# The fp4 network of a two-layer program: VectorE does the whole rounding of the wide row, and the turn is reordered

## The reference, cut to what matters

```python
def fp4_quant_dequant(x):               # blocks of 16 along the last dimension
    xb = x.reshape(shape[:-1] + (shape[-1] // BLOCK, BLOCK))
    scale = jnp.max(jnp.abs(xb), axis=-1, keepdims=True) / 6.0
    scale = jnp.maximum(scale, jnp.float32(1e-12))
    xn = xb / scale
    idx = jnp.searchsorted(_MID, jnp.abs(xn))
    q = _GRID[idx] * jnp.sign(xn) * scale
    return q.reshape(shape)

def fp4_linear(x, w):
    xq = fp4_quant_dequant(x)
    wq = fp4_quant_dequant(w)
    return jnp.einsum('bsk,nk->bsn', xq, wq)
gate = fp4_linear(x, w_gate)
y = fp4_linear(x, w_up)
h = jax.nn.silu(gate) * y
return fp4_linear(h, w_down)
```

## Time and profile before

| | us |
|---|---|
| median of 3 runs | 1154.24 |
| lowest and highest run | 1153.39 and 1157.0 |
| the profiled execution's own time | 1158.26 |
| its span | 1156.4 |
| VectorE busy | 795.2 (69%) |
| TensorE busy | 891.3 (77%) |
| GpSimd busy | 139.5 (12%) |

### The profile page before, as it was taken

One profiled execution on the slowest core, in us unless ns is written; L12 is line 12 of the kernel. 1 busy time (PEld: TensorE's weight loads), 2 busy tenths in 40 slices (PEclk: granted clock), 3 DMA queues, 4 the chain that ended last, 5 costly groups with the idle time before them and its releaser, 6 DMA issues. The chain is left out here.

```text
span 1156.4 us, 20054 instructions
## 1 busy us (share of the span) xinstructions
PE 891.3 (77%) x7220; PEld 502.5 (43%) x7220; DVE 795.2 (69%) x1440; ACT 439.1 (38%) x786; POOL 139.5 (12%) x108
## 2 busy tenths in 40 slices
PE   5429999999898866999735747999996984576774
PEld 4116766666565532433212313443434842343442
DVE  0762344788878885999978835878873333899982
ACT  3524666656545423554314540110112255222221
POOL 3520000000000001000004760000000000123231
PEclk8857999999989877999977888999998796787786
DMA  7400000000000001554341346665640000000000
GB/s 187 68 1 2 2 3 3 3 3 3 2 2 2 2 1 64 198 196 173 144 128 73 119 145 219 199 203 189 208 146 0 1 1 1 1 0 18 9 19 27
DMA packets 53988, 79.80 MB, mean 69 GB/s; under 512 B 14288, under 2 KB 28432, under 8 KB 53776
## 3 DMA queue, kind: packets, MB, share of 16 engines
q1 hardware_dynamic: 49680, 76.57, 20.9%
q10 hardware_dynamic: 4224, 2.10, 0.6%
HBM read 40.90 MB, written 35.65 MB: 66 GB/s over the span
## 5 line engine op out<-in xcount | busy, mean ns | idle before, releaser
L1466 PE MATMUL bank<-ex_hh,Wd 128*128 128x512 f32 x256 | 130.2, 601 | 7.3 <-DVE ex_hh L1527 7.3
L1163 ACT ACTIVATE so_u<-bank,bu 128x512 f32<-128x512 f32 x128 | 87.8, 686 | 113.0 <-PE bank L57 112.9
L1527 DVE TENSOR_TENSOR ex_hh<-ex_pg,bank 128x512 f32<-128x512 f32 x128 | 84.3, 673 | 46.4 <-DMA ex_pg<-hidden 26.9
L882 ACT ACTIVATE att_qk<-bank 128x512 f32<-128x512 f32 x128 | 66.8, 601 | 46.1 <-PE bank L712 45.6
L970 DVE TENSOR_TENSOR att_am<-bank,causal 128x512 f32<-128x512 f32 x64 | 44.0, 687 | 51.3 <-PE bank L746 51.2
L746 PE MATMUL bank<-att_qk 64*128 64x128 f32 x1024 | 78.2, 295 | 0.0
L1148 POOL TENSOR_TENSOR so_made<-so_u,so_g 128x512 f32<-128x512 f32 x33 | 54.7, 1672 | 193.9 <-ACT so_g L1169 188.2
L746 PEld LDWEIGHTS bank<-att_qk 64*128 64x128 f32 x1024 | 65.6, 196 | 20.8 <-issue 20.8
L1267 DVE SCALAR_TENSOR_TENSOR so_made<-bank,bg,so_u 128x512 f32<-128x512 f32 x95 | 68.9, 744 | 8.2 <-DMA hidden<-so_made 4.0
L1466 PEld LDWEIGHTS bank<-ex_hh,Wd 128*128 128x128 f32 x256 | 47.8, 192 | 57.6 <-issue 32.7
L55 PE MATMUL bank<-Hhi,Wgh 128*128 128x512 f16 x128 | 51.3, 401 | 27.0 <-DVE so_made L1267 14.8
(11 more groups left out here) (379 smaller groups left out, 1852.9 us busy)
## 6 DMA issues: line engine op xcount, KB each, us to landing
hidden<-so_made SPq DMA_DIRECT2D x128, 256.0 KB, 2.0
ex_pg<-hidden SPq DMA_DIRECT2D x64, 512.0 KB, 3.8
xin<-in_L_attn_x_dram ACTq DMA_DIRECT2D x8, 256.0 KB, 7.6
out_dram<-ff_ot SPq DMA_DIRECT2D x8, 256.0 KB, 2.3
so_other<-so_key SPq DMA_DIRECT2D x2, 512.0 KB, 5.5
wm<-in_L_wmod_dram SPq DMA_DIRECT2D x2, 384.0 KB, 5.8
F<-so_fhi SPq DMA_DIRECT2D x2, 256.0 KB, 4.0
F<-so_flo SPq DMA_DIRECT2D x2, 256.0 KB, 4.1
```

Of the source, the lines that this page charges most:

```text
L882: nc.scalar.activation(qk[t % 2][:, r, :, :].rearrange("p a l -> p (a l)"), psF[r], ACT.Relu).then_inc(s_["fe"], 1)
L1163: nc.scalar.activation(u[m % 4][:], psU[q][:, :], ACT.Silu, bias=bu[:, k:k + 1], scale=1.0 / WS).then_inc(s_u[q], 1)
L1466: nc.tensor.matmul(psY[j][:, :], Wd[:, n, :], hh[n % 4][:], start=False, stop=n == EBLK - 1).then_inc(s_dn[n % 4], 1)
L1527: nc.vector.tensor_tensor(hh[k % 4][:], pg[k // 2 % 4][:, k % 2, :], psW[k % 4][:, :], ALU.mult).then_inc(s_hh[k % 4], 1)
```

## The change

- The helper is cut in three: `fp4_normalise` (to the product with the reciprocal), `fp4_grid` (mask, constant, addition) and `fp4_scale` (subtraction, product with the scale). The narrow step of the scale becomes a `scalar_tensor_tensor` with a tile `tiny` of 1e-12 as second tensor. The narrow step L82 goes: its factor is applied in the product with the row, which becomes a `scalar_tensor_tensor` too. A rounding so has nine steps, not ten. `tiny` is filled by GpSimd in the chain of constants.
- In the fp4 network GpSimd has no work any more; VectorE does the subtraction and the scaling of the wide row directly after the grid step.
- VectorE's turn is reordered: wide rounding, gated 0 and 1, normalise x, gated 2, add_x, gated 3, then grid and scale of x. Before it was: wide rounding to the grid, gated 0 and 1, all of x's rounding, add_x, gated 2 and 3.
- TensorE: `by_token` waits only for the normalise step of the tile before and stands between gate_up 2 and gate_up 3; `out_by_token` comes before `hidden_back`; the three groups of `hidden_back` are spread between `quantised_back` and the gate_ups of the next tile but one; in the last turn they use three banks instead of one. ScalarE's order follows.

```diff
-def fp4_rounding(nc, step, src, n, w):
-    sc, rc, xn, m = w["sc"][:, 0:n // 16], w["rc"][:, 0:n // 16], w["xn"][:, 0:n], w["m"][:, 0:n]
+def fp4_normalise(nc, step, src, n, w):
+    sc, rc, xn = w["sc"][:, 0:n // 16], w["rc"][:, 0:n // 16], w["xn"][:, 0:n]
     step(nc.vector.tensor_reduce(sc, blocks(src), AX.X, ALU.max, apply_absolute_value=True))
-    step(nc.vector.tensor_scalar(sc, sc, 1.0 / 6.0, 1e-12, ALU.mult, ALU.max))
+    step(nc.vector.scalar_tensor_tensor(sc, sc, 1.0 / 6.0, w["tiny"][:, 0:n // 16], ALU.mult, ALU.max))
     step(nc.vector.reciprocal(rc, sc))
-    step(nc.vector.tensor_scalar(rc, rc, 1.0 - 2.0 ** -24, None, ALU.mult))
-    step(nc.vector.tensor_tensor(blocks(xn), blocks(src), by_block(rc), ALU.mult))
+    return nc.vector.scalar_tensor_tensor(blocks(xn), blocks(src), 1.0 - 2.0 ** -24, by_block(rc), ALU.mult, ALU.mult)
+def fp4_grid(nc, step, n, w):
+    xn, m = w["xn"][:, 0:n], w["m"][:, 0:n]
     step(nc.vector.tensor_scalar(m.bitcast(U32), xn.bitcast(U32), 0x7F800000, None, ALU.bitwise_and))
     step(nc.vector.tensor_scalar(m, m, 1.0, 1.5 * 2.0 ** 22, ALU.max, ALU.mult))
     return nc.vector.tensor_tensor(xn, xn, m, ALU.add)
+def fp4_scale(nc, step, dst, n, w):
     xn = w["xn"][:, 0:n]
-    step(fp4_rounding(nc, step, src, n, w))
     step(nc.vector.tensor_tensor(xn, xn, w["m"][:, 0:n], ALU.subtract))
     return nc.vector.tensor_tensor(blocks(dst), blocks(xn), by_block(w["sc"][:, 0:n // 16]), ALU.mult)
...
                         def by_token(t):
                             upto(pe, s_hs, t + 1)
-                            upto(pe, s_xq, t)
+                            upto(pe, s_xn, t)
...
-                        def hidden_back(t):
+                        def hidden_back(t, k, ps):
+                            n = NBLK[k]
                             upto(pe, s_hq, t + 1)
-                            for k, n in enumerate(NBLK):
+                            if ps is psT:
                                 upto(pe, s_e3, t * 3 + k)
...
                         def turn(t, follow, behind):                      # TensorE
                             if follow > 0:
                                 gate_up(t + 1, 2)
+                            if follow > 2:
+                                by_token(t + 3)
+                            if follow > 0:
                                 gate_up(t + 1, 3)
+                            if behind:
+                                out_by_token(t - 1)
+                            hidden_back(t, 0, psT)
                             if follow > 1:
                                 quantised_back(t + 2)
-                            if follow > 2:
-                                by_token(t + 3)
-                            hidden_back(t)
+                            hidden_back(t, 1, psT if follow > 0 else psH)
                             if follow > 1:
                                 gate_up(t + 2, 0)
+                            hidden_back(t, 2, psT if follow > 0 else psU[0])
+                            if follow > 1:
                                 gate_up(t + 2, 1)
                             down(t)
-                            if behind:
-                                out_by_token(t - 1)
...
                         def turn(t, ahead1, ahead2, behind):              # VectorE
                             quantise_hidden(t)
+                            scale_hidden(t)
                             if ahead1:
                                 gated(t + 1, 0)
                                 gated(t + 1, 1)
                             if ahead2:
-                                quantise_x(t + 2)
+                                normalise_x(t + 2)
+                            if ahead1:
+                                gated(t + 1, 2)
                             if behind:
                                 add_x(t - 1)
                             if ahead1:
-                                gated(t + 1, 2)
                                 gated(t + 1, 3)
+                            if ahead2:
+                                quantise_x(t + 2)
...
-                    @block.gpsimd
-                    def _(pool):
-                        with pool.Fori(0, NT) as t:
-                            xn, n = work_h["xn"], CH * I_FF
-                            pool.wait_ge(s_round, FIRST + t + 1)
-                            nc.gpsimd.tensor_tensor(xn[:], xn[:], work_h["m"][:], ALU.subtract).then_inc(s_grid, 1)
-                            pool.wait_ge(s_grid, FIRST + t + 1)
-                            pool.wait_ge(s_T3, FIRST + t * 3)
-                            nc.gpsimd.tensor_tensor(blocks(hq[:]), blocks(xn[:]), by_block(work_h["sc"][:]),
-                                                    ALU.mult).then_inc(s_hq, 1)
```

More of the change, by code:

```diff
@@ L148, in program @@
         eps_ln = sb("eps_ln", [P, 1])
+        tiny = sb("tiny", [P, ST // P * I_FF // 16])
         mod = sb("mod", [P, 2, 6, NB])
@@ L283, in program @@
             work |= {k: tb("prep_" + k, [P, QW // 16]) for k in ("sc", "rc")}
+            work["tiny"] = tiny
             xin = tb("xin", [P, 8, 4, P])
@@ L367, in _ @@
                     step(nc.gpsimd.memset(eps_ln[:], LN_EPS))
+                    step(nc.gpsimd.memset(tiny[:], 1e-12))
                     step(nc.gpsimd.memset(ones16[:], 1.0))
@@ L1738, in fp4_network @@
                 work_h |= {k: tb(k + "_h", [P, CH * I_FF // 16]) for k in ("sc", "rc")}
+                work_x["tiny"] = work_h["tiny"] = tiny
                 psH, psX, psT, psY = bank[0], bank[1], bank[6], bank[7]
@@ L1743, in fp4_network @@
                                              "T4", "e4", "out", "dve"))
-                s_round, s_grid = sem("ff_round"), sem("ff_grid")
+                s_xn, s_hn, s_round = (sem("ff_" + n) for n in ("xn", "hn", "round"))
                 def upto(eng, s, n):
@@ L1783, in gate_up @@
                             nc.tensor.matmul(psU[c % 2][:, 0:I_FF], x_c, wuT[:], start=True, stop=True).then_inc(s_GU, 1)
-                        def hidden_back(t):
+                        def hidden_back(t, k, ps):
+                            n = NBLK[k]
                             upto(pe, s_hq, t + 1)
-                            for k, n in enumerate(NBLK):
+                            if ps is psT:
                                 upto(pe, s_e3, t * 3 + k)
[L1789 to L1792, removed]
+                            for c in range(CH):
+                                at = c * I_FF + k * P
+                                m = nc.tensor.transpose(ps[0:n, c * P:(c + 1) * P], hq[:, at:at + n], ident[:])
+                            m.then_inc(s_T3, 1)
                         def down(t):
@@ L1853, in silu, with take_hidden @@
                             nc.scalar.activation(sg[c % 2][:], psG[c % 2][:, 0:I_FF], ACT.Silu).then_inc(s_sg, 1)
-                        def take_hidden(t):
+                        def take_hidden(t, k, ps):
+                            n = NBLK[k]
                             upto(act, s_Y, t)
-                            for k, n in enumerate(NBLK):
-                                upto(act, s_T3, t * 3 + k + 1)
-                                nc.scalar.copy(hqT[0:n, k, :], psT[0:n, :]).then_inc(s_e3, 1)
+                            upto(act, s_T3, t * 3 + k + 1)
+                            nc.scalar.copy(hqT[0:n, k, :], ps[0:n, :]).then_inc(s_e3, 1)
                         def take_out(t):
@@ L1877, in turn @@
                         def turn(t, follow, behind):
+                            if follow > 2:
+                                take_h(t + 3)
                             if follow > 0:
@@ L1912, in quantise_hidden, with scale_hidden @@
                             upto(dve, s_hq, t)
-                            fp4_rounding(nc, step, hh[:], CH * I_FF, work_h).then_inc(s_round, 1)
+                            fp4_normalise(nc, step, hh[:], CH * I_FF, work_h).then_inc(s_hn, 1)
+                            upto(dve, s_hn, t + 1)
+                            fp4_grid(nc, step, CH * I_FF, work_h).then_inc(s_round, 1)
+                        def scale_hidden(t):
+                            upto(dve, s_round, t + 1)
+                            upto(dve, s_T3, t * 3)
+                            fp4_scale(nc, step, hq[:], CH * I_FF, work_h).then_inc(s_hq, 1)
                         def add_x(t):
@@ L1922, in prologue @@
                         def prologue():
-                            quantise_x(0)
-                            quantise_x(1)
+                            for t in range(2):
+                                normalise_x(t)
+                                quantise_x(t)
                             for c in range(CH):
@@ L1944, in _ @@
                         with dve.Fori(0, NT - 3) as r:
-                            step = Chain(dve, s_dve, r, ROUNDING_STEPS + FP4_STEPS, FIRST + before)
+                            step = Chain(dve, s_dve, r, PER_TURN, FIRST + before)
```

(2 more changed lines are left out.)

34 lines of the change are left out of this document (22 added, 12 removed).

## The result

| | before | after |
|---|---|---|
| median of 5 runs, us | 1154.24 (1152.62 to 1157.0) | 1159.46 (1158.49 to 1160.71) |
| profiled execution: time, span | 1158.26, 1156.4 | 1159.46, 1157.8 |

The ratio after to before is 1.0044, with a 95% interval of 1.0027 to 1.0061: the change makes the kernel slower by about 5 us. The time lies in the forecast's own range (1153 to 1160), but above 1157.7, so the outcome that I held likeliest, no measurable change, is wrong. Medians in this document are of all runs; the ratios leave out one run of e6 (1417.93 us) and one of e8 (1728.37 us), which were slow.

A forecast was written before the change was run, and what follows sets the result against it. VectorE's queue was taken to set the network's turn. Terms of -1.6, +2.7, +5.4, +0.5, +2.2, -6.5 and -0.1 gave +2.6 us: 1160.9 profiled, median 1156.8 (+0.2%), own range 1153 to 1160, wider range 1149.5 to 1164.

The forecast's parts named there:

- no measurable change: Whole kernel: the median was forecast to stay between 1150.8 and 1157.7 us, chance 0.43.
- the fourth rival: Narrow steps of x stay slow for a reason other than GpSimd: about 1176 us, chance one in thirty.
- Prologue: Network before its first wide reduction: by_token(1) no longer waits for the whole first rounding, -1.6 us.
- turns 0, 5 and 6: Network's first turn and two late turns: slower in the new order, by +2.7, +0.5 and +2.2 us.
- turn 7: Last turn to span's end: earlier hq, three banks, down product partly at full clock, -6.5 us.
- the preparation: Edited helper before the network: narrow step still waits for GpSimd, -0.1 us; bound 5.6 us earlier.
- turns 1 to 4: Inner network turns: VectorE waits for silus, 21.1 us a turn against 19.76, +5.4 us together.
- my walk: Step-by-step path through one inner turn: 20.3 us at TensorE's full clock, 22.0 at half, 21.1 taken.
- the first rival: TensorE's half clock holds through gate_up 2, by_token and gate_up 3: 1163.9 us; slower side 0.38 with the fourth rival.
- The second rival: TensorE keeps the full clock in the network: -8.4 us, 1145.7; chance 0.19 together with the third rival.
- the step still ends at about 49.5: Preparation: the new two-tensor narrow step waits to the end of GpSimd's step, so only -0.1 us.
- The third rival: Two-tensor forms do not wait for GpSimd in the preparation: -5.6 us, 1151.3; chance one in twelve.

The follow-up runs named there:

- e6: Kernel after with twelve unread 352-column products on TensorE ahead of gate_up 2: 1170.12 us, ratio to before 1.0120.
- e8: Kernel after with the old turn order but its new last turn, GpSimd's two wide steps back in turns 0 to 6: 1142.70 us, ratio to before 0.9889.
- e4: Kernel before with only the new scalar_tensor_tensor forms, GpSimd's wide steps and old order kept: 1149.55 us, ratio to before 0.9942.
- e1: Kernel after with the old order on TensorE, ScalarE and VectorE, GpSimd still out of the stage: 1152.24 us, ratio to before 0.9973.
- e3: Kernel after with grid and scale of x moved ahead of the fourth gated product on VectorE: 1154.65 us, ratio to before 0.9995.
- e9: Kernel after with six unread 352-column products on TensorE ahead of gate_up 2: 1154.45 us, ratio to before 0.9990.
- e11: Kernel after, run again unchanged: 1160.45 us, ratio to before 1.0051.
- e7: Kernel after with the old rounding helper at the preparation's call alone: 1161.89 us, ratio to before 1.0051.

## Why the prediction was right in its steps and wrong in its class

**What held.** VectorE's queue set the turn, the narrow steps were slow because of GpSimd (0.19 us without it, and e4 and e8 show the waits return with it), so the fourth rival fell. VectorE's own work stayed level and a wait for the silus took the place of x's rounding. Prologue, turns 0, 5 and 6 were within 0.4 us, turn 7 within 1.0; there the down product was wholly at full clock, where I had taken part of it. That the sum came out so near, +2.6 for +2.8 measured in the two edited stretches, is luck: turns and prologue were 2.9 us worse than forecast, turn 7 was 1.0 and the preparation 1.7 better. The medians are 5.2 apart.

**The term that was mis-sized: turns 1 to 4**, put at +5.4 and measured at +7.35, 21.62 us a turn for 21.1. The turn shown ran at the half clock all through the exposed path, so my walk for that clock can be held against it. The third product started at 15.0 (I had 14.9), add_x ended at 16.2 (16.2), the second silu at 18.2 (18.4) and the fourth product at 18.8 (18.9). The step that was off is what stands behind the fourth product: I had 3.1 us for grid and scale of x, and the next wide reduction began after 3.58.
- *The end of the loop.* The wide reduction waits 0.51 us for `ff_xq` L96, which is now the last instruction of the loop's turn (turns 1 to 5 run in a loop on VectorE). I had 0.035, as between any two steps. In the kernel before, e1 and e3, whose turns end with a gated product, the gap there is 0.12; the old order has another 0.19 before add_x. That it is the loop's end that makes the wait so long is not shown by itself: the same wait was 0.33 behind turn 0 and 0.28 behind turn 5.
- *The clock was right on average only.* The walk has 1.4 us of waiting for silus at the full clock and 0.8 + 2.2 = 3.0 at the half one; 21.1 stands for 2.2. Measured were 2.3 a turn over turns 1 to 4, between 1.7 and 3.0, with a granted clock of 0.50 to 0.70 on the path. e9 puts the clock's part at 0.97 us a turn or more. TensorE was idle for 2.5 to 3.6 us before gate_up 2, and not for the 4 and more that I had reckoned.
- *The base was not all work.* I took 19.45 for VectorE's own work; that held the 0.48 us a turn for which the kernel before waits for silus. The walk's own steps come to 20.3 - 1.4 = 18.9, the measured turn without its silu waits to 19.3. The 0.4 between them is the end of the loop.

Against e1 the order cost 2.47 us a turn, 2.3 of waiting for silus and 0.2 of longer gaps, where the two numbers of mine have 21.1 - 19.45 = 1.65 between them.

The truth lay between the forecast and the first rival, past the point (21.3 us a turn) from which that rival was to decide, though the half clock held through the whole path only in some turns. What kept the time under its 1163.9 was, in the stage, turn 7, 2.5 us better than it had it, and turns 1 to 4, 1.65 better. The second rival, the full clock, is refuted by the granted clock of 0.50 to 0.70; e9, with the full clock there and gate_up 2 still 0.8 us late, has a turn of 20.65, half a microsecond of loop end included.

**The preparation**, put at -0.1 with -5.6 as the bound, was -1.8 (1.46 of it by the forms). The step that failed was "the step still ends at about 49.5". It waited, but not to the end. The third rival is neither right nor gone: the form waits less, and the mask step then waits in its place.

The Trainium skill's page "SBUF — State Buffer" (Who interferes with whom) calls the port pair that VectorE shares with GpSimd an exclusive lock, and says, where it speaks of VectorE's 2-port modes, that whoever issues first holds the pair for the whole instruction. I had carried that over to a form with two SBUF inputs. For GpSimd's two-tensor steps the rows of e4 agree (the narrow step ends at 1038.18, GpSimd's at 1038.13); for its one-tensor step in the preparation they don't: the two-tensor form was through 1.64 us before that step's end.

**What stays open.** Network and preparation together are +2.8 us; the spans differ by 1.4 in the first pair of profiles and 3.4 in the second, the medians by 5.2, within an interval of 3.1 to 7.0. The shorter middle of after (1.3 and 0.7 us) explains the first, and not the medians. Most single runs of the kernel before lie in two groups, 1151 to 1153 and 1155.5 to 1158.6, with a mean granted clock over the run of about 0.884 up to 1153.2 and 0.878 from 1155.5 on. The profiled ones were of the upper group; no run of the lower one has a profile, so where the groups part, and why, is not shown. I take the change's cost in the edited stages, 2.8 us, as shown, and the remainder of 0.3 to 4.2 us as not placed.

## What to carry to other kernels

When a reordering takes a queue's filler away from a place, walk the other engines' path through that place at the lowest clock that the profile shows after an idle stretch, and look at what is last in the loop: an instruction whose result the next turn's first step waits for costs there. Before taking a helping engine out, change the instruction forms alone: here two forms gave 0.6% (e4), and giving up GpSimd's help cost 0.5 us an inner turn of it back (e1). A change with a good and a bad half is best split: the old loop with GpSimd in it, the new last turn and the new forms (e8) beat both kernels by over 1%. When a step waits for another engine, measure from that engine's step and not from your own chain's start: 1.8 us here were 1.46.

## What the runs showed of the hardware that I had not expected

- A narrow scalar_tensor_tensor with both tensors in SBUF, issued during GpSimd's one-tensor step of 5.36 us, ended 3.72 us after that step's start, in the kernel after (43.52 to 47.24) and in e4 (43.76 to 47.48) alike, though it was issued 1.14 us into the step in the one and 0.37 in the other; a tensor_scalar in the same place waits to its end. Why 3.72 is not shown. The wide form of it at 47.90 ran at its own price, 1.33 us, while the GpSimd step was still under way.
- The granted clock's pattern is not noise. The turns of the kernel after were 21.95, 21.60, 21.06, 22.34, 21.48, 20.33, 17.03, and in e11 21.96, 21.59, 21.06, 22.34, 21.49, 20.31, 17.04, though the network started 0.9 us later. e7 has the same seven to 0.02. A spread between turns of 1.3 us can repeat to 0.02.
- A product of 352 fp32 columns took 0.6 us as two instructions at the full clock; unread products cost a full share of TensorE's queue, and six of them still paid for themselves against the kernel after (ratio to before 0.9990 for 1.0044).
